# Linear attention in a fused two-layer kernel: squares on ScalarE, and the division on 32x32-transposed blocks

## The reference

```
def softmax_kernel_features(data, proj, is_query):        # proj is 44 x 16
    data_dash = einsum('bhnd,md->bhnm', data / d ** 0.25, proj)
    diag_data = sum(square(data), axis=-1, keepdims=True) * 0.5 / sqrt(d)
    stab = max over m of data_dash (queries), or its maximum over everything (keys)
    return ratio * (exp(data_dash - diag_data - stab) + 1e-4)

q, k, v = heads of x @ W_qkv
q1, k1 = features of q and of k
kv, ksum = einsum('bhnm,bhnd->bhmd', k1, v), sum(k1, axis=2)
out = einsum('bhnm,bhmd->bhnd', q1, kv) / einsum('bhnm,bhm->bhn', q1, ksum)
return out @ W_proj + b_proj
```

## Time and profile before

| | |
|---|---|
| median of 3 runs | 2345.42 us (2343.82 to 2352.02) |
| the profiled execution | 2344.25 us, its span 2342.5 us |
| TensorE busy (matmul) | 1865.3 us, 80% of the span |
| VectorE busy | 1399.9 us, 60% |
| ScalarE busy | 1074.8 us, 46% |
| mean granted TensorE clock | 0.847 of full speed |

### The profile page before, as it was taken

One profiled execution on the slowest core, in us unless ns is written; L12 is line 12 of the kernel. 1 busy time (PEld: TensorE's weight loads), 2 busy tenths in 40 slices (PEclk: granted clock), 3 DMA queues, 4 the chain that ended last, 5 costly groups with the idle time before them and its releaser, 6 DMA issues. The chain is left out here.

```text
span 2342.5 us, 30986 instructions
## 1 busy us (share of the span) xinstructions
PE 1865.3 (80%) x9804; PEld 1002.0 (43%) x9804; DVE 1399.9 (60%) x2512; ACT 1074.8 (46%) x1903; POOL 443.5 (19%) x603
## 2 busy tenths in 40 slices
PE   3868888967877461777759876999899993999998
PEld 2745655545433330000012225444133432888887
DVE  4558449966201576999968886999845553122121
ACT  1100312213110485999979985333187771222221
POOL 5000000000111001222210003333004344233333
PEclk8979999988988585555569997999599996999999
DMA  3010110006699002434211014878676752677774
GB/s 87 1 43 27 48 39 28 18 4 243 275 410 375 21 0 74 148 107 128 65 33 41 27 27 85 125 126 128 77 88 102 100 106 101 191 199 207 209 202 107
DMA packets 153248, 258.88 MB, mean 111 GB/s; under 512 B 28624, under 2 KB 124737, under 8 KB 148134
## 3 DMA queue, kind: packets, MB, share of 16 engines
q1 hardware_dynamic: 134870, 239.15, 38.6%
q0 software_dynamic: 18256, 18.19, 4.0%
HBM read 215.55 MB, written 57.91 MB: 117 GB/s over the span
## 5 line engine op out<-in xcount | busy, mean ns | idle before, releaser
L1745 PE MATMUL ps<-arena 128*128 x384 | 196.8, 617 | 106.3 <-ACT ps L1787 58.6
L1787 ACT ACTIVATE ps<-ps,arena 128x512 f32<-128x512 f32 x384 | 256.7, 1120 | 6.3 <-POOL arena L1771 6.3
L1755 DVE TENSOR_REDUCE arena<-ps 128x1024 f32 x192 | 232.7, 1225 | 24.5 <-PE ps L1745 12.2
L1787 ACT ACTIVATION_READ_ACCUMULATOR ps<-ps,arena 128x1 f32 x384 | 234.7, 668 | 0.0
L2162 DVE TENSOR_REDUCE arena<-ps 128x1024 f32 x192 | 221.4, 1220 | 9.2 <-PE ps L2408 6.6
L2631 ACT ACTIVATE arena<-ps 128x1024 f32<-128x1024 f32 x192 | 185.7, 1021 | 88.7 <-PE ps L2509 87.0
L2968 ACT ACTIVATE arena<-ps,arena 128x256 f32<-128x256 f32 x234 | 89.5, 481 | 236.8 <-PE ps L2933 236.8
L1952 ACT ACTIVATE arena<-ps 128x1024 f32<-128x1024 f32 x192 | 178.7, 1046 | 7.9 <-DVE arena L1972 4.6
L2408 PE MATMUL ps<-arena 96*128 96x512 bf16 x500 | 162.6, 430 | 23.3 <-DVE arena L2162 12.1
L531 PE MATMUL ps<-arena 96*128 96x456 f32 (+1 forms) x512 | 170.0, 482 | 8.8 <-DMA arena<-la_xt 5.2
L2988 DVE TENSOR_TENSOR arena<-ps,arena 128x384 f32<-128x384 f32 x39 | 21.8, 558 | 257.3 <-PE ps L2944 257.3
(11 more groups left out here) (393 smaller groups left out, 3151.9 us busy)
## 6 DMA issues: line engine op xcount, KB each, us to landing
arena<-in_sm_w_dram SPq DMA_DIRECT2D x128, 576.0 KB, 15.4
arena<-in_re_w_dram SPq DMA_DIRECT2D x39, 1252.0 KB, 5.8
arena<-ra_parts SPq DMA_DIRECT2D x192, 192.0 KB, 9.1
routed_in<-routed_in SPq DMA_DIRECT2D x8, 3332.0 KB, 14.0
ra_parts<-arena SPq DMA_DIRECT2D x48, 192.0 KB, 2.4
arena<-routed_in SPq DMA_DIRECT2D x39, 196.0 KB, 5.4
arena<-la_xt SPq DMA_DIRECT2D x16, 384.0 KB, 3.4
arena<-arena SPq DMA_DIRECT2D x64, 96.0 KB, 2.2
```

The source lines that it names most:

```text
L1745: ins = pe.matmul(ps[:, 2 * (n % 4) + t % 2, :], QM[j][:, h, t * P:(t + 1) * P], KI[:, b, h // HG, :], start=True, stop=True)
L1755: v.tensor_reduce(MXq[:, b, 2 * u:2 * u + 2, at_head(h)], ps[:, 2 * (n % 4):2 * (n % 4) + 2, :], AX.X, ALU.max).then_inc(s_lk, 1)
L1787: ins = act.activation(bank, bank, ACT.Exp, bias=nb[n % 4][:, t % 2:t % 2 + 1], scale=c_reg, accum_out=RS[:, b, t, at_head(h):at_head(h) + 1])
```

## The change

`squares` is new: ScalarE squares the 192 values of a tile out of the accumulator into SBUF (function Square), with a signal of its own (`ksq`, `qsq`). VectorE's `squared_lengths` keeps only the sum over each head, and its wait for the products becomes a wait for the squares. In the k pass ScalarE's loop becomes: square 0, square 1, copy of the next batch's transposed rows, square 2, square 3, with the last two batches written out. In the q pass ScalarE issues, on step t, the square of tile t+1 (on step 3 that of tile 0 of the next batch), then exp of tile t, then the copy of turn t-1; the last two batches are written out as well. VectorE's `normalise` transposes both banks in blocks of 32x32 into SBUF, so that queries lie along the partitions and the 16 equal denominators of a head side by side; it takes the reciprocal of one of them per head and query (128 x 32), multiplies with it spread over 16, and transposes back.

```diff
--- before.py
+++ after.py
@@ -532,19 +532,20 @@
                                 Wx[:, kind, c, at:at + w], start=(c == 0), stop=(c == NC - 1))
         ins.then_inc(done.sem, 1)
 
+    def squares(act, b, t, products_done, squared):
+
+        products_done.wait(act, b, t + 1)
+        act.activation(SQ[t % 2], ps[:, 2 * (t % 2), 0:D], ACT.Square).then_inc(squared.sem, 1)
+
     def squared_lengths(v, link, t):
-
-        q = ps[:, 2 * (t % 2), 0:D]
-        link(v.tensor_copy(SQ[t % 2], q))
-        link(v.tensor_tensor(SQ[t % 2], SQ[t % 2], q, ALU.mult))
         link(v.tensor_reduce(dg[t % 2], SQ[t % 2].rearrange("p (h d) -> p h d", h=NH), AX.X, ALU.add))
 
     features = lambda t: ps[:, 2 * (t % 2):2 * (t % 2) + 2, D:D + FH].rearrange("p g (h f) -> p g h f", h=6)
     by_head = lambda a: a.rearrange("p (g h) -> p g h", g=2)[:, :, :, None].to_broadcast([P, 2, 6, NF])
 
 
-    xn, xt, xc, kp, kd = S1("rows_normed"), S1("rows_turned"), S1("rows_turned_copied"), \
-        S1("k_products", T, T + 1), S1("k_features", T, 2)
+    xn, xt, xc, kp, ksq, kd = S1("rows_normed"), S1("rows_turned"), S1("rows_turned_copied"), \
+        S1("k_products", T, T + 1), S1("k_squared", T), S1("k_features", T, 2)
     s_lk, s_mx, s_gm, s_ns = (sem(f"la_{n}") for n in ("k_chain", "row_max", "global_max", "guard_ready"))
     s_xs = [sem(f"la_turned_rows{j}_stored") for j in range(2)]
 
@@ -563,9 +564,9 @@
                 ins.then_inc(xn.sem, 1)
 
             def batch(b, ahead):
-                link = Link(v, s_lk, b * (3 * T))
+                link = Link(v, s_lk, b * T)
                 for t in range(T):
-                    kp.wait(v, b, t + 1)
+                    ksq.wait(v, b, t + 1)
                     squared_lengths(v, link, t)
                     v.tensor_reduce(MX[:, bass.ds(b, 1), t], features(t), AX.XYZ, ALU.max)
                     v.scalar_tensor_tensor(
@@ -592,15 +593,31 @@
         @block.scalar
         def _(act):
             xc.start(act)
+            ksq.start(act)
             for j in range(2):
                 act.sem_inc(s_xs[j], 1)
-            with act.Fori(0, B // 2) as i:
+
+            def turned_copy(b, i, j):
+                xt.wait(act, b, 1)
+                prev(act, kp, i, j)
+                act.wait_ge(s_xs[j], 16 * i + 1)
+                act.activation(XTs[j], ps[0:DC, 4:6, :], ACT.Copy).then_inc(xc.sem, 1)
+
+            turned_copy(0, 0, 0)
+            with act.Fori(0, B // 2 - 1) as i:
                 for j in range(2):
-                    b = 2 * i + j
-                    xt.wait(act, b, 1)
-                    prev(act, kp, i, j)
-                    act.wait_ge(s_xs[j], 16 * i + 1)
-                    act.activation(XTs[j], ps[0:DC, 4:6, :], ACT.Copy).then_inc(xc.sem, 1)
+                    squares(act, 2 * i + j, 0, kp, ksq)
+                    squares(act, 2 * i + j, 1, kp, ksq)
+                    turned_copy(2 * i + j + 1, i + j, 1 - j)
+                    squares(act, 2 * i + j, 2, kp, ksq)
+                    squares(act, 2 * i + j, 3, kp, ksq)
+            for b in (B - 2, B - 1):
+                squares(act, b, 0, kp, ksq)
+                squares(act, b, 1, kp, ksq)
+                if b == B - 2:
+                    turned_copy(B - 1, B // 2 - 1, 1)
+                squares(act, b, 2, kp, ksq)
+                squares(act, b, 3, kp, ksq)
 
         @block.sync
         def _(sp):
@@ -768,9 +785,9 @@
     Q1T = [g4(2 * NF, [6, S]) for _ in range(2)]
     QD = [g4(P, [2 * FH]) for _ in range(2)]
     KX = [g4(2 * NF, [2, 6, 2, HD]) for _ in range(2)]
-    RD, OT = g4(P, [S]), g4(P, [2, S])
-    qp, qd, qe, qt, qc = S1("q_products", T, T + 1), S1("q_features", T, 2), S1("q_exp", T, 2), \
-        S1("q_turned", T, 2), S1("q_turned_copied", T, 2)
+    SUMS, RD, TN, OT = g4(P, [S]), g4(P, [S // 32, 2]), g4(P, [S]), g4(P, [2, S])
+    qp, qsq, qd, qe, qt, qc = S1("q_products", T, T + 1), S1("q_squared", T), S1("q_features", T, 2), \
+        S1("q_exp", T, 2), S1("q_turned", T, 2), S1("q_turned_copied", T, 2)
     num, ot, pr, hh = S1("read_out", 2, 3), S1("normalised", 2), S1("projected"), S1("stream_updated")
     s_qk, s_rd = sem("la_q_chain"), sem("la_reciprocal")
     xq = [sem(f"la_q_rows{j}_loaded") for j in range(2)]
@@ -796,12 +813,9 @@
             def chain(b, link, t):
 
                 j = t % 2
-                qp.wait(v, b, t + 1)
-                q = ps[:, 2 * j, 0:D]
-                v.tensor_copy(SQ[j], q)
-                link(v.tensor_reduce(mq[j].rearrange("p (g h) -> p g h", g=2), features(t), AX.X, ALU.max))
-                link(v.tensor_tensor(SQ[j], SQ[j], q, ALU.mult))
-                link(v.tensor_reduce(dg[j], SQ[j].rearrange("p (h d) -> p h d", h=NH), AX.X, ALU.add))
+                qsq.wait(v, b, t + 1)
+                v.tensor_reduce(mq[j].rearrange("p (g h) -> p g h", g=2), features(t), AX.X, ALU.max)
+                squared_lengths(v, link, t)
                 link(v.scalar_tensor_tensor(out=dg[j], in0=dg[j], scalar=0.125, in1=mq[j], op0=ALU.mult,
                                             op1=ALU.add))
                 qt.wait(v, b, t - 1)
@@ -810,10 +824,14 @@
 
             def normalise(b, half):
                 rows = slice(0, P if half == 0 else D - P)
+                turned = TN[rows].rearrange("p (n k d) -> p n k d", k=2, d=HD)
+                link = Link(v, s_rd, 8 * b + 4 * half)
                 num.wait(v, b, half + 1)
-                v.reciprocal(RD[rows], ps[rows, 6, :]).then_inc(s_rd, 1)
-                v.wait_ge(s_rd, 2 * b + (half + 1))
-                v.tensor_tensor(OT[rows, half, :], ps[rows, 7, :], RD[rows], ALU.mult).then_inc(ot.sem, 1)
+                link(v.transpose(SUMS[rows], ps[rows, 6, :]))
+                link(v.transpose(TN[rows], ps[rows, 7, :]))
+                link(v.reciprocal(RD[rows], SUMS[rows].rearrange("p (n k d) -> p n k d", k=2, d=HD)[:, :, :, 0]))
+                link(v.tensor_tensor(turned, turned, RD[rows][:, :, :, None].to_broadcast(list(turned.shape)), ALU.mult))
+                v.transpose(OT[rows, half, :], TN[rows]).then_inc(ot.sem, 1)
 
             def add(b):
                 rows = m.H[:, bass.ds(b, 1), :, :].rearrange("p o (a t) d -> p (o a) t d", t=2)
@@ -826,7 +844,7 @@
                                m.H[:, bass.ds(b, 1), t, :].rearrange("p o d -> p (o d)"))
 
             def batch(b, behind, last_behind):
-                link = Link(v, s_qk, b * (4 * T))
+                link = Link(v, s_qk, b * (2 * T))
                 chain(b, link, 0)
                 if last_behind:
                     add(b - 2)
@@ -849,21 +867,31 @@
 
         @block.scalar
         def _(act):
-            for s in (qe, qc):
+            for s in (qsq, qe, qc):
                 s.start(act)
-            with act.Fori(0, B // 2) as i:
+
+            def batch(b, i, j, ahead):
+                prev(act, num, i, j)
+                for t in range(T + 1):
+                    if t < T - 1:
+                        squares(act, b, t + 1, qp, qsq)
+                    elif t == T - 1 and ahead:
+                        squares(act, b + 1, 0, qp, qsq)
+                    if t < T:
+                        qd.wait(act, b, t + 1)
+                        act.activation(QD[t % 2], QD[t % 2], ACT.Exp).then_inc(qe.sem, 1)
+                    if t:
+                        qt.wait(act, b, t)
+                        act.activation(Q1T[j][:, :, (t - 1) * P:t * P].rearrange("p (g a) q -> p g a q", g=2),
+                                       ps[0:2 * NF, 4:6, 0:3 * P].rearrange("p g (a q) -> p g a q", a=3),
+                                       ACT.Identity, bias=little[0:2 * NF]).then_inc(qc.sem, 1)
+
+            squares(act, 0, 0, qp, qsq)
+            with act.Fori(0, B // 2 - 1) as i:
                 for j in range(2):
-                    b = 2 * i + j
-                    prev(act, num, i, j)
-                    for t in range(T + 1):
-                        if t < T:
-                            qd.wait(act, b, t + 1)
-                            act.activation(QD[t % 2], QD[t % 2], ACT.Exp).then_inc(qe.sem, 1)
-                        if t:
-                            qt.wait(act, b, t)
-                            act.activation(Q1T[j][:, :, (t - 1) * P:t * P].rearrange("p (g a) q -> p g a q", g=2),
-                                           ps[0:2 * NF, 4:6, 0:3 * P].rearrange("p g (a q) -> p g a q", a=3),
-                                           ACT.Identity, bias=little[0:2 * NF]).then_inc(qc.sem, 1)
+                    batch(2 * i + j, i, j, True)
+            batch(B - 2, B // 2 - 1, 0, True)
+            batch(B - 1, B // 2 - 1, 1, False)
 
         @block.tensor
         def _(pe):
```

## The result

| | before | changed |
|---|---|---|
| median, 5 runs each | 2348.76 us (2343.82 to 2357.22) | 2363.10 us (2358.16 to 2367.96) |
| span of the profiled execution | 2342.5 us | 2356.4 us |

What follows compares the result with a forecast made beforehand. VectorE's cycle was taken to set the q pass's pace. K pass -5.2, holds +12.8 and clock falls +13.6 gave +21.2 us: a span near 2364 and a median of 2366.5 us, range 2343 to 2383.

Steps and rivals of the forecast that it cites:

- K pass: K pass: chain 0.40 us shorter and 0.25 us waits for L571 gone, per batch; -5.2 us, bounds 3 to 7.
- VectorE in the q pass: Q pass: chain about 2.0 us instead of 2.70, division 3.25 instead of 3.99, cycle 16.8 instead of 21.5; no longer sets pace.
- Holds: Q pass: exp and copy queue behind the waiting square, TensorE idles 1.86 us; +1.60 us a batch, +12.8 for eight.
- the two turns named: Turns 1 and 3 in the q pass: each starts 4.45 us after the start of products instead of 2.42, +2.03.
- the other three steps of the list: Q pass, per batch: turn 2 -1.10 us, turn 0 unchanged, projection after turn 3 -1.36 us.
- Clock: Q pass: half of 16 holds let TensorE's clock fall, 1.7 us each; +13.6 us, bounds 0 and 31.
- eleven idles: Idles of 1.68 to 2.58 us in the trace before; the clock fell within 2 us of six, not for five.
- Tail: End of q pass: gives back 2 x 0.74 plus a little over 1 us, cancelling the first two batches' extra loss.
- Rival 1: Q pass: the hold is there but the clock stays at full; +7.6 us, 2353 us, chance 0.27.
- rival 2: Q pass: ScalarE isn't late, TensorE's own steps bound it; -25.5 us with the k pass, 2320 us, chance 0.08.
- rival 3: Q pass: Square and Exp switch ScalarE's function table 8 times a batch; 82 us, 2435 us, chance 0.03.

Runs made afterwards that it cites:

- old_division: The changed kernel with the division of before (reciprocal of 128x512); ratio 1.0070 to the kernel before.
- square_between: The changed kernel with ScalarE's q-pass square issued after exp and ahead of the copy; ratio 0.9970 to the kernel before.
- square_last: The changed kernel with ScalarE's q-pass square issued after both exp and the copy; ratio 0.9895 to the kernel before.
- filled_hold: The changed kernel with extra, thrown-away matmuls on TensorE in the idles ahead of turns 1 and 3; ratio 0.9998 to the kernel before.
- square_last_old_division: square_last with the division of before; ratio 0.9989 to the kernel before.
- division_alone: The kernel before with the new division only, squares staying on VectorE in both passes; ratio 0.9942 to the kernel before.

## Why the prediction was right, and where it was off

Direction, range and mechanism held. Foreseen were 2366.5 us against a median of before of 2345.4, +21.2; measured are +14.3 by medians and +13.9 by span. Part of that agreement is luck: of the 13.9, the passes that the sum speaks of, k and q, gave 10.6, half of what was foreseen for them, and 4.0 came from the stages behind them, which the change doesn't touch.

- **K pass.** Foreseen -5.2, with 3 to 7 as bounds; measured -6.9. The chain is 0.40 shorter as worked out, but the wait before the transposes shrank by 0.34 and the others added up to about 0.5, not 0.25: I counted one wait for the release of the banks per batch, where the products of two of the four tiles had one each.
- **VectorE in the q pass.** Held. A division took 3.24 to 3.27 us (3.25 foreseen) and a chain 1.91 (2.0 foreseen), and it ceased to set the pace; old_division shows that this alone brings nothing there.
- **Holds.** Foreseen idle 1.86, measured 1.83, ahead of the two turns named; the other three steps of the list behaved as written (turn 2 and the projection follow without idle). The sum is 1.36 a batch instead of 1.60, in part because turn 3 is held 1.74 in every second batch, and the pass from one projection to the next products takes 2.62 instead of 2.72. square_between and square_last show that it is the queue's order and nothing else about the square.
- **Clock.** Foreseen eight falls at 1.7 us, 13.6; the profile has six, 10.2. The price was right, the number a guess from eleven idles. filled_hold shows that the falls cost what they seem to: 8.2 us for five.
- **Tail.** I let it cancel against the first two batches. It did not: up to the first projection the pass lost 9.3 us (two falls in it), and after the last but one it won back 4.7, in part because the projection there ran at full speed, where it had been low before.

The term that was mis-sized is the q pass: 26.4 foreseen, 17.6 measured, 3.4 of it in the count of falls, 1.9 in the holds (0.24 in each of eight batches), and the remaining 3.5 in the first two batches, the last one and the tail. Rival 1 (no falls) is refuted for this execution, rival 2 is what square_last became, and of rival 3 there is no trace: the changed passes have no table load beyond those that before had.

## What to carry to other kernels

Moving work to an engine that is idle three quarters of the time, as ScalarE is in this pass, costs nothing in busy time and can still cost the kernel: ask what stands behind the new instruction in that engine's queue, and whether its wait comes before or after the point at which the rest was due. Here four lines further down were worth 1.7% of the time. And a part that gains by itself (the division, 0.58%) gains nothing that can be measured behind another part's wait, and in full (2 x 0.74 us a batch) once that wait is gone; test parts alone and in both orders.

## What the runs showed of the hardware

An idle of 1.82 or 1.83 us in an otherwise dense stream let TensorE's clock fall in six of the q pass's thirteen cases, for 3.4 us each time; idles of 1.29 in the same places of square_between's steady batches never did. In square_last_old_division the clock fell behind two idles of 1.59 us ahead of a projection, and not behind one of 1.65. Matmuls whose result is thrown away, put into the idle, kept the clock at the full level and made the whole kernel about 0.5% faster than the change without them (0.46% by medians, 0.63% by ratios). And a low stretch can be long: in square_last_old_division the granted clock averaged 0.53 over 18 us in which TensorE was busy 17.5 us, so work alone did not bring it back at once; why that one lasted five times as long as the 3.4 us of the others stays open. In the tails of square_last and division_alone it stayed low for over 45 us, there with TensorE busy about half the time (27.1 and 27.2 of 50 us).
